# Keys turned through a memory scratch and a block turn on VectorE instead of on TensorE

## The chip, the cores and the metric

The kernel runs on one core of a Trainium2 chip. The time is the device time of one execution in microseconds; lower is better. Engines are called TensorE (PE, its weight loads PEld), VectorE (DVE), ScalarE (ACT), GpSimd (POOL) and SyncE (SP), which only issues DMAs here.

## The reference, cut to what matters

Input x has 16 sequences of 256 tokens with 512 features, in float32. Two stages follow each other, both with a gate and a residual:

```
k = layernorm(x)                       # per token, over 512 features
# per channel, over the 256 tokens of a sequence (a recurrence in time):
#   a <- decay * a + exp(k) * v ;  b <- decay * b + exp(k)
#   y = (a_prev + e2*exp(k)*v) / (b_prev + e2*exp(k))        v = ctx
x = x + tanh(g_xattn) * y
h = layernorm(x)
x = x + tanh(g_ffn) * (shared_mlp(h) + moe_top2_of_8(h))
```

Layernorm goes over features, so it wants tokens on the partitions. The recurrence goes over tokens, so it wants channels on the partitions and time along the row. Keys k and values v must therefore be transposed on the way in (tokens x channels to channels x tokens), and y on the way back.

## The kernel before

Tokens are cut into 32 tiles of 128 (512 features each); two tiles, one sequence, are a unit. The body walks over units 0 to 15 (and -2 and -1 as a lead-in without matmuls of the shared MLP); each unit has 11 steps, one for each 128-wide block of the shared MLP's hidden layer. Units 2 to 11 are a hardware loop of two units per turn, the others are written out. In step s of unit u TensorE makes `up_pair(u, s)` (24 matmuls, L1024) and, up to unit 13, `down_block(u-1, s-1)` (6 matmuls, L1057). Behind each `up_pair` stand ScalarE's Silu (L834), VectorE's product (`hidden`, L1311), ScalarE's rounding to float16 (`hidden_hi`, L850) and GpSimd's remainder (`hidden_lo`, L634). The Silu writes one of three staging buffers (`srng`) and waits until `hidden_lo` of three blocks earlier has read it; three PSUM buffers PU are used in turn too.

The attention stages of later units run in the same steps. Which step is written in the table `STAGE_AT`: for each stage, the offset in steps from the unit's own start, first and second tile. `-18` means 18 steps ahead, which is step 4 two units earlier. Every engine walks through the same steps and does its part of each stage in a fixed order within the step, so an instruction that waits holds back all that stands behind it on its engine. The stages of a tile:

- `stats_x`: VectorE's mean and variance of x (L1229, L1231); GpSimd's `inv_std` (L579, L581, L583) behind it in the same step.
- `norm_k`: ScalarE writes the normalised tile to `kbuf` (L798), the only such buffer.
- `turn_k`: TensorE transposes `kbuf` into PSUM bank PT with four matmuls (L948), ahead of the `up_pair` of its step; ScalarE's `exp_k` (L804) reads PT. PT is shared with the turned y.
- `factors` (GpSimd L595, L599), `turn_v` (values; by TensorE for the first two units, later from a load in blocks and VectorE's L1264), `den` (VectorE L1253 and the scan L1257; GpSimd's `add_den` L606), `num` (VectorE L1269 and the scan L1271; GpSimd's `add_num` L611), `divide` (VectorE L1276, L1279).
- `turn_y`: TensorE transposes y (L948) behind 18 of the 24 matmuls of an `up_pair`; it waits for `divide`. Then `add_y` (VectorE L1284), `norm_x2` (ScalarE L813, L814), `split_x` (VectorE L1293).
- SyncE turns and stores the row (`turn_and_store`, L422, L424), loads x two units ahead (L399); the transposed row is xT, which `logits` (TensorE L993) and `up_pair` read. `choose` (VectorE L1298 to L1305) picks the experts.

Of every second unit, the even ones from 2 on, GpSimd also sends eight indirect stores in steps 8, 9 and 10 (`send_slots`, L618: two, two and four), behind its `add_den` or `add_num` of that step. In unit 0 SyncE also loads the down weights (step 3 to 5) and writes 2560 KB of zeros to memory (L471, step 7). In units 12 to 14 VectorE and ScalarE also split weights of the first expert. From 767 us on come the experts' tiles.

How ctx comes in blocks already, for all units from 2 on (one DMA per quarter q of the partitions, four per tile, runs of 32 words):

```
sp.dma_start(ctxb[r][q * SQ:(q + 1) * SQ, :].rearrange("p (k b j) -> p k b j", k=KT, j=SQ),
             ctx_rows[bass.ds(c * P, P), :].rearrange("(b i) (k q j) -> q i k b j", i=SQ, k=KT, j=SQ)[q])
dve.transpose(PR[:, :], ctxb[k])
```

The load swaps 32x32 blocks, and VectorE's transposition, which turns each 32x32 block in itself, does the rest.

Of the kernel before, what the change touches and what calls it, by code (L numbers as in the profile page):

```python
# [9 lines left out]
P = 128  # L10
# [42 lines left out]
SQ = 32  # L53
# [4 lines left out]
STAGE_AT = {  # L58
    "stats_x": (-21, -16),
    "norm_k": (-19, -13),  # L60
    "turn_k": (-18, -12),
    "factors": (-16, -10),
    "turn_v": (-16, -10),
    "den": (-14, -9),
# [68 lines left out]

def tiles_at(stage, u, s):
    return [(u.shift(-(o // JT)), k) for k, o in enumerate(STAGE_AT[stage])
            if o % JT == s and u.shift(-(o // JT)).exists()]
# [6 lines left out]
def build(nc, x, ctx_in, g_x, g_f, t_decay, t_first, router, w_ug, w_dn, s_ug, s_dn, out):  # L143
    es = ExitStack()
    with es:
# [10 lines left out]
        moe_d = nc.dram_tensor("moe_d", (NTOK + 4 * P, D), F32, kind="Internal").ap()  # L156
        slot_d = nc.dram_tensor("slot_d", (TRASH + TOPK * NTOK, 2), F32, kind="Internal").ap()
# [155 lines left out]
        bn_done = [sem(f"bn{n}") for n in range(2)]; inv_done = [sem(f"inv{n}") for n in range(2)]  # L313
        k_norm = sem("k_norm"); k_turned = sem("k_turned"); v_turned = sem("v_turned"); v_used = sem("v_used")
# [76 lines left out]
        def _(sp):  # L391
# [8 lines left out]

            def load_ctx(c, r):
                if isinstance(c, int) and c < UT * PE_TURNED:
                    sp.dma_start(ctxb[r], ctx_rows[bass.ds(c * P, P), :]).then_inc(v_in[r], 16)
                else:
                    for q in range(P // SQ):
                        sp.dma_start(ctxb[r][q * SQ:(q + 1) * SQ, :].rearrange("p (k b j) -> p k b j", k=KT, j=SQ),
                                     ctx_rows[bass.ds(c * P, P), :].rearrange("(b i) (k q j) -> q i k b j", i=SQ, k=KT, j=SQ)[q]
                                     ).then_inc(v_in[r], 16)
# [39 lines left out]
            def unit(u, first=0):  # L448
                for s in range(first, JT):
                    if s == 1 and not (u.fixed and not 2 <= u.v < FIRST_HELD + 2):  # L450
                        start_sums(u.shift(-2))
                    for v, k in tiles_at("turn_v", u, s):
                        if v.shift(1).exists():
                            wait_alone(v_turned, v.tile(k) + 1)
                            load_ctx(v.tile(k) + 2, k)
                    for m in W_LOAD_AT.get(key(u, s), ()):
                        load_u(m)
                    for v, k in tiles_at("split_x", u, s):
                        turn_and_store(v, k)
                        if v.shift(2).exists():  # L460
                            if u.fixed and u.v in (1, 2):
                                sp.wait_ge(wd_lo, 5 if u.v == 1 and k == 0 else 6 if u.v == 1 else JT)
                                sp.wait_ge(wu_lo, JT)
                            load_x(v.shift(2), k)
                    if key(u, s) in EARLY_LOAD_AT:
                        load_chunk(0, EARLY_LOAD_AT[key(u, s)])
# [296 lines left out]
        def _(act):  # L763
# [91 lines left out]
            def unit(u, first=0, also=None):  # L855
                for s in range(first, JT):
# [4 lines left out]
                    for v, k in tiles_at("turn_k", u, s):  # L861
# [83 lines left out]
        def _(pe):  # L945
# [116 lines left out]
            def unit(u, first=0):  # L1062
                for s in range(first, JT):
                    for v, k in tiles_at("turn_k", u, s):
                        turn_k(v, k)

                    def attend():
                        for v, k in tiles_at("turn_v", u, s):
                            if v.fixed and v.v < PE_TURNED:
                                turn_v(v, k)  # L1070
# [125 lines left out]
        def _(dve):  # L1196
# [68 lines left out]

            def num(u, k):
# [165 lines left out]
            def unit(u, first=0, also=None):  # L1432
                for s in range(first, JT):
# [18 lines left out]
                    for v, k in tiles_at("split_x", u, s):  # L1452
                        split_x(v, k)
                    for v, k in tiles_at("divide", u, s):
                        divide(v.tile(k))
# [8 lines left out]
                    for v, k in tiles_at("turn_v", u, s):  # L1464
                        if not (v.fixed and v.v < PE_TURNED):
                            turn_v(v, k)
# [119 lines left out]
```

## Time and profile before

| | us |
|---|---|
| median of 3 runs | 1230.34 (1228.75 to 1232.13) |
| profiled execution, its own time | 1232.66 |
| its span, first to last instruction | 1230.9 |
| TensorE busy | 1163.2 (94%) |
| VectorE busy | 682.7 (55%) |
| GpSimd busy | 653.7 (53%) |
| ScalarE busy | 509.6 (41%) |
| TensorE's matmuls of unit 0, unit 1 begin | 50.57, 96.06 |
| last up_pair ends, about | 767 |

A timeline row gives the start, the time, the engine, the line, the operation, the tile written and those read, and in brackets how long the engine was idle before and which instruction ended that. Names are those of the allocation: `wkv` stands for all the attention buffers. One row can hold several instructions in a row of the same line (x4). Offsets are us from the span's start.

### The profile page before, as it was taken

What the parts mean: (1) busy time and instruction counts of PE and PEld (TensorE: products, weight loads), DVE (VectorE), ACT (ScalarE), POOL (GpSimd) and SP (SyncE); (2) the same over time, 40 slices, a digit from 0 to 9 for tenths busy, and PEclk for the clock granted to TensorE, in tenths of its full rate; (3) what the DMA queues carried; (4) which work ended last, traced back from release to release, by engine and by line L of the source; (5) the groups of instructions that cost most, each with busy time, mean ns of one, the idle gap of its engine ahead of it and who ended that gap; (6) DMA issues with size and microseconds to landing.
All of it is one profiled execution on the core that took longest, in us unless ns stands there. A gap on an engine that the chain in (4) does not pass through costs nothing. (4 is left out here: it accounts for less than half of the span.)

```text
span 1230.9 us, 25978 instructions
## 1 busy us (share of the span) xinstructions
PE 1163.2 (94%) x8396; PEld 817.2 (66%) x8396; DVE 682.7 (55%) x1357; ACT 509.6 (41%) x915; POOL 653.7 (53%) x754
## 2 busy tenths in 40 slices
PE   1478999999999999999999989999999999999998
PEld 1366777777777777777776767566666666666653
DVE  6776787786786777776777866222222223222112
ACT  5665444443544443544534443333333333333220
POOL 7887457367457457456557542344444444444320
PEclk9998999999999999999999989999999999999999
DMA  8373232232222222222332323999899989997738
GB/s 234 92 206 72 53 70 53 53 69 52 54 66 52 60 61 55 68 49 60 87 69 48 59 65 62 204 178 180 173 169 172 176 171 165 178 169 130 127 50 319
DMA packets 232773, 136.29 MB, mean 111 GB/s; under 512 B 176477, under 2 KB 201077, under 8 KB 232544
## 3 DMA queue, kind: packets, MB, share of 16 engines
q1 hardware_dynamic: 213792, 97.55, 34.3%
q0 software_dynamic: 18048, 37.47, 17.6%
q8 instruction: 51, 0.84, 0.3%
q14 instruction: 50, 0.41, 0.1%
q10 hardware_dynamic: 832, 0.02, 0.0%
HBM read 69.83 MB, written 44.97 MB: 93 GB/s over the span
## 5 line engine op out<-in xcount | busy, mean ns | idle before, releaser
L1024 PE MATMUL PU<-xT,wreg 128*128 128x256 f16 x4224 | 504.5, 276 | 0.4 <-DVE srng L1311 0.4
L1024 PEld LDWEIGHTS PU<-xT,wreg 128*128 128x128 f16 x4224 | 415.1, 99 | 74.8 <-DVE srng L1311 0.7
L753 POOL DMA_INDIRECT moe_d<-wkv,acc x71 | 112.0, 1578 | 217.2 <-ACT wkv L928 214.2
L1131 PE MATMUL PU<-acc,wkv 128*128 x1284 | 214.5, 312 | 0.0
L1057 PE MATMUL PD<-wreg,hreg 128*128 128x512 f16 x858 | 206.4, 379 | 0.0
L634 POOL TENSOR_TENSOR hreg<-srng,hreg 128x256 f16<-128x256 f32 x165 | 134.6, 822 | 73.9 <-ACT hreg L850 72.9
L1131 PEld LDWEIGHTS PU<-acc,wkv 128*128 128x128 f16 x1284 | 125.1, 97 | 69.4
L1545 DVE TENSOR_TENSOR wkv<-PR,wkv 128x384 f16<-128x384 f32 x71 | 39.6, 557 | 208.1 <-ACT wkv L922 148.7
L1152 PE MATMUL PD<-acc,wkv 128*128 (+1 forms) x639 | 149.6, 379 | 1.5 <-DVE wkv L1545 1.5
L834 ACT ACTIVATE srng<-PU 128x256 f32<-128x256 f32 x176 | 66.7, 379 | 201.4 <-PE PU L1024 149.5
L1057 PEld LDWEIGHTS PD<-wreg,hreg 128*128 128x128 f16 x858 | 84.0, 98 | 73.5
L850 ACT ACTIVATE hreg<-srng 128x256 f16<-128x256 f32 x176 | 72.5, 412 | 118.5 <-DVE srng L1311 117.1
L1311 DVE SCALAR_TENSOR_TENSOR srng<-PU,srng 128x256 f32<-128x256 f32 x176 | 72.5, 412 | 85.2 <-ACT srng L834 72.2
L1152 PEld LDWEIGHTS PD<-acc,wkv 128*128 128x128 f16 (+1 forms) x639 | 62.5, 98 | 67.7 <-issue 1.7
L1276 DVE RECIPROCAL wkv<-wkv 128x512 f32<-128x512 f32 x32 | 106.9, 3340 | 0.3
L928 ACT ACTIVATE wkv<-PD,acc 128x512 f32<-128x512 f32 x71 | 48.8, 687 | 106.6 <-PE PD L1152 81.4
L618 POOL DMA_INDIRECT slot_d<-stw,sidx x64 | 68.4, 1068 | 23.0 <-issue 15.8
L918 ACT ACTIVATE wkv<-PU 128x352 f32<-128x352 f32 x71 | 32.9, 463 | 113.4 <-PE PU L1131 47.2
L948 PE MATMUL PT<-ident,wkv 128*128 128x128 f32 x256 | 42.5, 292 | 38.9 <-ACT wkv L798 27.8
L606 POOL TENSOR_TENSOR wkv<-wkv 128x512 f32<-128x512 f32 x32 | 44.4, 1387 | 58.8 <-DVE wkv L1257 58.8
L1131 PE MATMUL PL<-acc,wkv 128*128 x420 | 68.4, 313 | 0.0
L948 PEld LDWEIGHTS PT<-ident,wkv 128*128 128x128 f32 x256 | 32.1, 149 | 48.4 <-ACT wkv L798 30.1
(177 smaller groups left out, 1327.5 us busy)
## 6 DMA issues: line engine op xcount, KB each, us to landing
wreg<-in_L_ffn_w_up_gate SPq DMA_DIRECT2D x48, 176.0 KB
acc<-in_x SPq DMA_DIRECT2D x32, 256.0 KB, 3.0
xhl_d<-wkv SPq DMA_DIRECT2D x32, 256.0 KB, 2.3
wkv<-in_ctx SPq DMA_DIRECT2D x112, 64.0 KB, 2.4
moe_d<-acc SPq DMA_DIRECT2D x13, 512.0 KB
out<-moe_d SPq DMA_DIRECT2D x2, 3328.0 KB, 21.1
acc<-n_L_ffn_shared_w_up_gate SPq DMA_DIRECT2D x16, 256.0 KB, 5.7
wreg<-in_L_ffn_w_down SPq DMA_DIRECT2D x12, 256.0 KB
```

The source lines that it names most:

```text
L618: pool.indirect_dma_start(out=slot_d, out_offset=bass.IndirectOffsetOnAxis(ap=sidx[:, 2 * (r.at + t) + k:2 * (r.at + t) + k + 1], axis=0), ...
L634: pool.tensor_tensor(hh[:, u.par, m, 1, :], srng[:, r, :], hh[:, u.par, m, 0, :], ALU.subtract).then_inc(hlo_ready, 1)
L753: pool.indirect_dma_start(out=moe_d, out_offset=bass.IndirectOffsetOnAxis(ap=didx[:, t:t + 1], axis=0), in_=ostage[t % 3], in_offset=None, ...
L834: act.activation(srng[:, r, :], PU[r][:, 0:UN], ACT.Silu, scale=1.0 / WS).then_inc(silu_done, 1)
L850: act.activation(hh[:, buf, m, 0, :], srng[:, r, :], ACT.Copy).then_inc(hhi_ready, 1)
L948: mm = pe.transpose(dst[:, kt * P:(kt + 1) * P], src[:, kt * P:(kt + 1) * P], ident[:, :])
L1024: mm = pe.matmul(PU[r][:, gu * UN:(gu + 1) * UN], sU[:, m, gu, a, kt, :], xT[:, u.par, b, kt, :], start=(kt == 0 and a + b == 0), stop=(kt ...
L1057: mm = pe.matmul(PD[t][:, :], hh[:, u.par, j, a, t * P:(t + 1) * P], sD[:, j, b, :], start=(j == 0 and a + b == 0), stop=(j == JT - 1 and ...
L1131: mm = pe.matmul(up_set[t % 2][gu][:, 0:I], xgT[:, t % 4, a, kt, :], weights(h, ((gu * 2 + b) * KT + kt) * I, P, I), start=(kt == 0 and a ...
L1152: mm = pe.matmul(PD[t % 2][:, :], ehT[0:M, t % 2, a, m * P:(m + 1) * P], weights(h, UW + (m * 2 + b) * D, M, D), start=(m == 0 and a + b = ...
L1276: dve.reciprocal(nd[:, 1], nd[:, 1]).then_inc(rcp_done, 1)
L1311: dve.scalar_tensor_tensor(out=srng[:, r, :], in0=PU[r][:, UN:2 * UN], scalar=HS / WS, in1=srng[:, r, :], op0=ALU.mult, op1=ALU.mult).then ...
```

## The change

From unit 2 on, keys take another way. `norm_k` writes `kbuf` as before. SyncE stores it to a scratch `k_d` in memory (`store_k`) and, when that has landed, loads it back into `kbuf` with its 32x32 blocks swapped (`load_k`, four DMAs, the same shape as for ctx). VectorE then turns the blocks into PT (`turn_k`), and `exp_k` reads PT as before. The four matmuls of `turn_k` on TensorE stay for units 0 and 1 alone. y is still turned by TensorE.

The longer way gets more steps: `stats_x`, with `inv_std`, moves from -21, -16 to -24, -20, `norm_k` from -19, -13 to -23, -18, and the key's turn from -18, -12 to -19, -13. `exp_k` keeps its step. The loads of ctx go one step later. In steps of the unit in which they run: `stats_x` from 1 and 6 to 9 and 2, `norm_k` from 3 and 9 to 10 and 4, the key's turn from 4 and 10 (TensorE) to 3 and 9 (VectorE). Units 0 and 1 keep the old table as `FIRST_AT`.

```diff
+FIRST_AT = {                       # units 0 and 1: the table of before
     "stats_x": (-21, -16), "norm_k": (-19, -13), "turn_k": (-18, -12),
+    "exp_k": (-18, -12), "load_v": (-16, -10), "store_k": (), "load_k": (),
...
 STAGE_AT = {
+    "stats_x": (-24, -20),
+    "norm_k": (-23, -18),
+    "store_k": (-23, -18),
+    "load_k": (-22, -17),
+    "turn_k": (-19, -13),
+    "exp_k": (-18, -12),
     "factors": (-16, -10),
     "turn_v": (-16, -10),
+    "load_v": (-15, -9),
...
+        k_d = nc.dram_tensor("k_d", (P, D), F32, kind="Internal").ap()
...
+            def load_blocks(buf, rows, landed):
+                for q in range(P // SQ):
+                    sp.dma_start(buf[q * SQ:(q + 1) * SQ, :].rearrange("p (k b j) -> p k b j", k=KT, j=SQ),
+                                 rows.rearrange("(b i) (k q j) -> q i k b j", i=SQ, k=KT, j=SQ)[q]).then_inc(landed, 16)
+            def store_k(c):
+                wait_alone(k_norm, c + 1)
+                sp.dma_start(k_d, kbuf).then_inc(k_out, 16)
+            def load_k(c):
+                wait_alone(k_out, 16 * (c + 1 - UT * PE_TURNED))
+                load_blocks(kbuf, k_d, k_in)
...
# SyncE, order within a step: start_sums, load_k, load_v, weights, turn_and_store with load_x, store_k, other loads
...
# TensorE
                     for v, k in tiles_at("turn_k", u, s):
-                        turn_k(v, k)
+                        if turned_by_pe(v):
+                            turn_k(v, k)
...
# VectorE, order within a step: hidden, add_y, choose, stats_x, split_x, turn_k, divide, den, num, turn_v
+            def turn_k(c):
+                wait_alone(k_in, 64 * (c + 1 - UT * PE_TURNED))
+                dve.wait_ge(x2_done, c - 1)
+                dve.transpose(PT[:, :], kbuf).then_inc(k_turned, 1)
```

## Rows read from the trace of the kernel before

**Rows 1.** TensorE's waits, whole span: line waited for, us in total, times, longest

```profile
PE PT L948 <- DVE wkv L1279: 11.1, 7, 3.5
```

**Rows 2.** busy us by stretch: PE, PEld, DVE, ACT, POOL, PEclk, DMA share, GB/s

```profile
426.00:471.00 45.00, 45.00 (x363) 34.30 (x361) 32.36 (x65) 18.06 (x33) 30.06 (x37) 1.00 0.25 59
```

**Rows 3.** timeline of TensorE, units 8 and 9: start, us, what

```profile
438.26 0.60 PE L948 MATMUL PT<-ident,wkv 128*128 128x128 f32 x4
...
456.31 0.60 PE L948 MATMUL PT<-ident,wkv 128*128 128x128 f32 x4
456.74 1.15 PE L1024 MATMUL PU<-xT,wreg 128*128 128x256 f16 x9
...
483.47 0.60 PE L948 MATMUL PT<-ident,wkv 128*128 128x128 f32 x4
```

**Rows 4.** timeline of VectorE, units 8 and 9, idle before in brackets

```profile
435.30 0.69 DVE L1279 TENSOR_TENSOR wkv<-wkv 128x512 f32<-128x512 f32 x1
...
437.46 0.17 DVE L1298 TENSOR_REDUCE lt<-PL 128x8 f32<-128x16 f32 x1 [1.13 <-PE PL L993]
...
444.03 0.69 DVE L1229 BATCH_NORM_STATS2 bn<-acc 128x6 f32 x1 [0.26 <-issue]
...
445.02 0.73 DVE L1264 STREAM_TRANSPOSE PR<-wkv 128x512 f32<-128x512 f32 x1
...
467.72 0.42 DVE L1311 SCALAR_TENSOR_TENSOR srng<-PU,srng 128x256 f32<-128x256 f32 x1 [4.48 <-ACT srng L834]
...
482.41 0.69 DVE L1279 TENSOR_TENSOR wkv<-wkv 128x512 f32<-128x512 f32 x1
```

**Rows 5.** timeline of GpSimd, unit 8 and the start of 9

```profile
445.50 0.22 POOL L579 TENSOR_SCALAR ve<-mv 128x1 f32<-128x1 f32 x1
...
446.58 0.27 POOL L583 TENSOR_SCALAR nmr<-mv,rstd 128x1 f32<-128x1 f32 x1 [0.21 <-POOL rstd L581]
...
452.20 1.18 POOL L606 TENSOR_TENSOR wkv<-wkv 128x512 f32<-128x512 f32 x1 [4.01 <-DVE wkv L1257]
...
457.28 1.18 POOL L611 TENSOR_TENSOR wkv<-wkv 128x512 f32<-128x512 f32 x1
...
466.53 1.30 POOL L634 TENSOR_TENSOR hreg<-srng,hreg 128x256 f16<-128x256 f32 x2
```

**Rows 6.** timeline of ScalarE, unit 8 step 8

```profile
451.30 0.38 ACT L834 ACTIVATE srng<-PU 128x256 f32<-128x256 f32 x1 [1.36 <-PE PU L1024]
```

**Rows 7.** two waits of TensorE and the granted clock (PEclk) behind them

```profile
66.39 0.66 PE L948 MATMUL PT<-ident,wkv 128*128 128x128 f32 x4 [1.31 <-ACT wkv L798]
...
73.62 0.79 PE L948 MATMUL PT<-ident,wkv 128*128 128x128 f32 x4 [1.80 <-DVE wkv L1279]
...
66.00:67.00 1.00, 0.61 (x6) 1.00 0.00 0
...
74.00:75.00 1.00, 1.00 (x7) 0.51 1.01 373
```

**Rows 8.** timelines of units -1 to 1: GpSimd, ScalarE, SyncE's queue, TensorE

```profile
51.52 1.18 POOL L611 TENSOR_TENSOR wkv<-wkv 128x512 f32<-128x512 f32 x1 [1.17 <-DVE wkv L1271]
...
48.92 0.58 ACT L804 ACTIVATE wkv<-PT 128x512 f32<-128x512 f32 x1
...
56.82 0.38 ACT L834 ACTIVATE srng<-PU 128x256 f32<-128x256 f32 x1 [3.98 <-PE PU L1024]
...
83.05 0.64 SPq L471 DMA_DIRECT2D moe_d<-hreg  x1
...
95.82 0.38 PE L993 MATMUL PL<-rt_w,xT 128*128 128x16 f16 x8 [6.52 <-DMA xT<-wkv]
```

**Rows 9.** DMA issues (KB each, median us to landing) and SyncE's issue time

```profile
xhl_d<-wkv SPq DMA_DIRECT2D x32, 256.0 KB, 2.3
wkv<-in_ctx SPq DMA_DIRECT2D x112, 64.0 KB, 2.4
...
473.80 2.98 SPq L406 DMA_DIRECT2D wkv<-in_ctx  x4
```

More of the change, by code:

```diff
@@ L57 @@
 LOOP = (1, 6)
-STAGE_AT = {
+FIRST_AT = {
     "stats_x": (-21, -16),
@@ L61 @@
     "turn_k": (-18, -12),
+    "exp_k": (-18, -12),
     "factors": (-16, -10),
     "turn_v": (-16, -10),
+    "load_v": (-16, -10),
+    "den": (-14, -9),
+    "num": (-13, -8),
+    "divide": (-12, -7),
+    "turn_y": (-11, -6),
+    "add_y": (-10, -5),
+    "norm_x2": (-9, -4),
+    "split_x": (-8, -3),
+    "logits": (-6, -1),
+    "choose": (-6, 1),
+    "store_k": (), "load_k": (),
+}
+STAGE_AT = {
+    "stats_x": (-24, -20),
[3 more added lines that the diff above has]
+    "turn_k": (-19, -13),
+    "exp_k": (-18, -12),
+    "factors": (-16, -10),
+    "turn_v": (-16, -10),
+    "load_v": (-15, -9),
     "den": (-14, -9),
@@ L131, with turned_by_pe @@
 LAST = [Route(GROUPS - 1, 14 * (GROUPS - 1), TILES - GT, UT, 0), Route(GROUPS, 14 * (GROUPS - 1) + 12, TILES - UT, UT, UT)]
+def turned_by_pe(u):
+    return u.fixed and u.v < PE_TURNED
 def tiles_at(stage, u, s):
-    return [(u.shift(-(o // JT)), k) for k, o in enumerate(STAGE_AT[stage])
-            if o % JT == s and u.shift(-(o // JT)).exists()]
+    found = []
+    for table, first in ((FIRST_AT, True), (STAGE_AT, False)):
+        for k, o in enumerate(table[stage]):
+            v = u.shift(-(o // JT))
+            if o % JT == s and v.exists() and turned_by_pe(v) == first:
+                found.append((v, k))
+    return found
 def key(u, s):
@@ L404, in load_ctx @@
                 else:
[L405 to L408, printed above, removed]
+                    load_blocks(ctxb[r], ctx_rows[bass.ds(c * P, P), :], v_in[r])
             def load_u(m):
@@ L451, in unit @@
                         start_sums(u.shift(-2))
-                    for v, k in tiles_at("turn_v", u, s):
+                    for v, k in tiles_at("load_k", u, s):
+                        load_k(v.tile(k))
+                    for v, k in tiles_at("load_v", u, s):
                         if v.shift(1).exists():
@@ L464, in unit @@
                             load_x(v.shift(2), k)
+                    for v, k in tiles_at("store_k", u, s):
+                        store_k(v.tile(k))
                     if key(u, s) in EARLY_LOAD_AT:
@@ L860, in unit @@
                         norm_k(v.tile(k))
-                    for v, k in tiles_at("turn_k", u, s):
+                    for v, k in tiles_at("exp_k", u, s):
                         exp_k(v.tile(k))
@@ L1453, in unit @@
                         split_x(v, k)
+                    for v, k in tiles_at("turn_k", u, s):
+                        if not turned_by_pe(v):
+                            turn_k(v.tile(k))
                     for v, k in tiles_at("divide", u, s):
@@ L1464, in unit @@
                     for v, k in tiles_at("turn_v", u, s):
-                        if not (v.fixed and v.v < PE_TURNED):
+                        if not turned_by_pe(v):
                             turn_v(v, k)
```

3 lines of the change are left out of this document (2 added, 1 removed).

## Prediction

> **What bounds the kernel now.** I first read the waits of TensorE, where the one for VectorE's y is the row to see [rows 1], and the busy table by stretches [rows 2]. In the loop TensorE has no gap at all: 45.00 of 45.00 us busy in a stretch of one unit, with VectorE at 32.36. All its large waits lie in units -2 to 1 and from unit 12 on. So any work taken off TensorE in units 1 to 13 is worth its full time, as long as nothing else ends last. I then read the timelines of each engine over unit 8 (matmuls from 416.94 us) and unit 9 (from 462.15), to see how far the other engines are from ending last, and found one place where they almost do. In step 5 of unit 9 TensorE starts to turn y at 483.47 [rows 3]; VectorE finished that y (L1279, 0.69 us) at 483.10 [rows 4]. The reserve is 0.37 us. The same place repeats in units 3, 5, 7, 9 and 11 (five times) with 0.23 to 0.37 us; step 5 of even units has 2.3 (438.26 against 435.99 [rows 3, 4]) and step 0 about 4.
>
> What makes this y late, followed back from 483.10: VectorE works without a real pause from 467.72, where it waited 4.48 us for the Silu [rows 4]. The Silu waited for the staging buffer that GpSimd's L634 frees at 466.53 + 0.65, and GpSimd was busy without a pause from 452.20 (`add_den` of step 8, then eight indirect stores of unit 8 with `add_num` among them) [rows 5]. That `add_den` waited until 452.20 for VectorE's scan, and VectorE had worked through from 437.46, where it last waited for TensorE, for the logits of unit 8 [rows 4]. From there to the y: 45.64 us. TensorE's own way between the same points: 46.01 us. The kernel has two nearly equal bounds.
>
> **The change part by part.**
>
> *Removed from TensorE:* 28 key turns, for tiles 4 to 31, made in units 0 to 13. One is 0.44 us of TensorE's time: it starts at 456.31 and the next matmul at 456.74 (0.43 to 0.44 wherever it stands) [rows 3]. Two per unit make 0.88 us, and 1.76 per pair of units. If TensorE stays the bound everywhere, 28 x 0.44 = 12.3 us.
>
> *Added to VectorE:* 28 block turns in steps 3 and 9. The same form exists for ctx: 0.73 us, and it holds the next instruction off for 0.63 to 0.73 [rows 4]. I take 0.65, with 0.95 as upper end for its two waits.
>
> *Moved:* `stats_x` leaves steps 1 and 6 for steps 9 and 2. On VectorE it holds 1.2 us (from the end of the one before to the transposition behind it, 443.8 to 445.02 [rows 4]). On GpSimd the three instructions of `inv_std` go with it, 1.35 us (445.50 to 446.85 [rows 5]). `norm_k` moves to steps 10 and 4 on ScalarE.
>
> *Along the late chain of a pair* (even unit 8, odd unit 9), against the times of before:
> VectorE, unit 8 steps 5 to 8: logits 0.44 earlier (one turn gone), `stats_x` gone from step 6, 1.2. The scan releases `add_den` at 450.55 instead of 452.20.
> VectorE, step 9: it must wait for the Silu of step 8, which starts at 451.30 [rows 6], now 0.44 earlier, so 451.3 for its product; then 0.3 product, 1.1 `stats_x`, 0.7 block turn, 0.7 multiply, 1.5 scan: 455.6. GpSimd, shifted with its `add_den`, is ready for `add_num` at 455.6 too: 1.6 earlier than 457.28 [rows 5].
> GpSimd then has `inv_std` of step 9 ahead of six indirect stores: +1.35. The staging buffer is free 0.25 us earlier than before.
> VectorE, unit 9 steps 1 to 4: step 1 loses `stats_x` and step 2 gains it, 0; step 3 gains the turn, +0.65.
> y is done at 483.10 - 0.25 + 0.65 = 483.5. TensorE, three key turns lighter, arrives at 483.47 - 1.32 = 482.15. It waits about 1.4 us (up to 1.7 with the dearer turn). The pair gains 1.76 - 1.4 = 0.3 us, where TensorE alone promised 1.76. The next y turns keep over 1 us of reserve (unit 8 step 5: 438.26 against 435.99 + 0.65).
> Five pairs, units 2 to 11: -1.5 us.
> Unit 1 has no indirect stores before it and 0.9 us of reserve: -0.88 + 0.2 = -0.7.
> Units 12 and 13: VectorE splits expert weights there too and TensorE waits for it already. The y turns of unit 13 step 5 and unit 14 step 0 are set by VectorE, +0.45 and +0.65: +1.1 together.
>
> *The first units.* Tile 4 now passes `norm_k` in unit -1 step 10, on ScalarE ahead of `exp_k` of tile 3, which it delays. GpSimd can give tile 4 its `inv_std` only behind `add_num` (51.52, now a `stats_x` of VectorE later, 52.6) [rows 8]: 53.8 + 1.35 = 55.1. ScalarE stands until then and has 0.8 us of `norm_k`, so `exp_k` of tile 3 goes from 48.92 to 55.9, 7.0 later. Behind it stand weight splitting and the first Silu, which had 3.98 us of idle time before it at 56.82 [rows 8]: it comes 3.0 later. VectorE's `stats_x` gone from step 1 gives a little back, so I take 2.7 us for tile 3's way. It ends in the transposition of its row into xT, for which TensorE waits 6.52 us at 95.82, because it stands behind the 2560 KB store of zeros issued at 83.05 [rows 8]. SyncE issues that store after its new waits (`store_k`, `load_k` behind the down weights), 1.5 to 3.2 us later. The wait swallows what the two turns gone from unit 0 save. I take +2.7, bounds 0 and +5.
>
> *SyncE and the DMA engines.* Per key tile one store and four loads more, 140 DMAs. A store of this size lands in 2.3 us, a ctx piece in 2.4; its four issues take 3.0 [rows 9]. The round trip is about 0.4 + 2.3 + 3.0 + 2.4 = 8.1 us, against 17 us from `norm_k` in step 10 (about 459) to the turn in step 3 (476). It is hidden; 0, and if the cover were gone the surplus would land on VectorE.
>
> **Sum:** -1.5 - 0.7 + 1.1 + 2.7 = +1.6 us. The profiled execution took 1232.66 with a span of 1230.9, the median of the runs is 1230.34; I add the sum to the median: 1232.0.
>
> **The rivals.**
> *Full gain.* VectorE's chain doesn't end last, because its turn or `inv_std` slips into pauses. For it: VectorE is busy only 72% of a unit [rows 2]. Against: the pauses lie outside this chain. Then 26 x 0.44 = 11.4 less 2.7 at the start: 1221.6. With half the wait: 1226.
> *The wait costs the clock too (slower).* After a wait of 1.31 us the granted clock stayed at 1.00, 2.4 GHz; after one of 1.80 us it fell to about 0.5, 1.2 GHz, and stayed there until 77.4 (the first of these us) [rows 7], which loses 1.7 us of work. My forecast of 1.4 to 1.7 lies between. From about 1.8 us of wait it decides: +1.7 in six pairs, 10 us: 1242. For it: each 0.1 us on the chain is in the wait. Against: the middle of my sum is nearer to 1.31.
> *The change doesn't do what it says for time:* the key trip comes late and VectorE stands in step 3. It needs twice the 8.1 us; each us late is 1 us per unit, 14 us: 1246.
>
> **How the numbers follow.** No difference, chain eats the gain: 0.47, own range 1227 to 1236. Full or half gain: 0.25. Clock falls in several pairs: 0.2. Late keys: 0.03. A dearer start alone (+5 or more): 0.05. The range for 8 in 10 reaches to 1222 and 1242. A measurement of this kernel tells 0.3%, 3.7 us, from no change. Faster: the gain cases and a little of the first, 0.28. Slower: clock, late keys, start and the upper edge of the first, 0.28. Within 0.3%: 0.44.
>
> **What would show it.** TensorE: 112 of the 272 matmuls of L948 gone; a wait "TensorE on L1279's line" of 1.2 to 1.7 us in step 5 of every odd unit from 3 on, none in the loop before; the spacing of two units 90.2 instead of 90.5. VectorE: 28 more transpositions of 0.73, now 56. Start: first matmul of unit 1 at 98 to 99 instead of 96.06. Wrong, if no such waits stand in the loop (then 1222), or if the granted clock shows 0.5 there (then 1242), or if VectorE waits for the key loads.

## The result: 29 us slower, and the profile after

| | before | after |
|---|---|---|
| median of six runs each | 1231.39 us | 1260.30 us |
| lowest to highest | 1228.75 to 1234.17 | 1258.53 to 1261.72 |
| span of the profiled execution | 1230.9 us | 1256.8 us |

The ratio is 1.0233, with a 95% interval of 1.0216 to 1.025. The time lies outside the range of 1222 to 1242 us. The profiled execution of the changed kernel took 1258.53 us. Lines have moved: turns by TensorE are L998, router logits L1043, up blocks L1074, down blocks L1107; VectorE's turn of ctx is L1315 and that of the keys L1320, the last multiplication of y L1335, `split_x` L1349, the second scan L1327; Silu is L884; GpSimd's `inv_std` is L629 to L633, `add_den` L656, an indirect store L668, `hidden_lo` L684.

TensorE's waits over the whole span (line waited for, us in total, times, longest):

```profile
PE PT L998 <- DVE wkv L1335: 29.9, 12, 4.7
PE PT L998 <- ACT wkv L848: 26.3, 4, 9.4
PE PL L1043 <- DMA xT<-wkv: 19.8, 7, 6.0
PE PU L1074 <- DVE srng L1367: 9.5, 8, 1.9
```

The wait for y went from 11.1 us [rows 1] to 29.9, and a wait of the up blocks for VectorE's hidden product, L1367, has come up that was 0.4 us before. The timeline of TensorE shows where both stand, here in unit 8's step 5 and in unit 9:

```profile
452.17 0.65 PE L998 MATMUL PT<-ident,wkv 128*128 128x128 f32 x4
...
478.11 0.82 PE L1074 MATMUL PU<-xT,wreg 128*128 128x256 f16 x6
480.08 2.79 PE L1074 MATMUL PU<-xT,wreg 128*128 128x256 f16 x24 [1.15 <-DVE srng L1367]
...
500.80 0.65 PE L998 MATMUL PT<-ident,wkv 128*128 128x128 f32 x4 [2.58 <-DVE wkv L1335]
```

Every pair of units in the loop has these two waits: 1.15 us at up block 1 of the odd unit (480.08) and about 2.55 us at the y turn of its step 5 (500.80, against 483.47 without a wait before [rows 3]). Even the y turn of step 5 of unit 8, which had 2.3 us of reserve [rows 3, 4], now starts only at 452.17, 0.13 us after its y.

The y turns of step 5 of units 3, 5, ..., 13 give the account, before and after: 212.04 and 217.62; 302.52 and 310.96; 393.00 and 405.90; 483.47 and 500.80; 573.95 and 594.02; 666.57 and 691.98. So 5.6 us are lost by unit 3, 14.5 in four pairs of the loop, 5.3 in units 12 and 13, and 0.5 behind them: 25.9 us, the difference of the two profiled spans. The medians differ by 28.9, because the profiled execution of the changed kernel was its fastest, and that of the kernel before, 1232.66 us, lay above its median. A pair of units was 90.48 us; now it is 93.2 to 93.3, or 94.9.

The difference between these two is the clock. Busy us by stretch (PE, PEld, DVE, ACT, POOL), PEclk, DMA share and GB/s, behind the y turn at 405.90 and behind the one at 500.80:

```profile
406.00:407.00 1.00, 1.00 (x10) 0.88 (x10) 0.59 (x5) 0.42 (x1) 0.37 (x1) 0.92 0.34 54
407.00:408.00 1.00, 1.00 (x4) 0.45 (x3) 0.49 (x3) 0.38 (x1) 1.00 (x2) 0.50 0.50 79
408.00:409.00 1.00, 1.00 (x4) 0.38 (x3) 0.96 (x2) 0.42 (x1) 1.00 (x2) 0.50 0.57 90
409.00:410.00 1.00, 1.00 (x5) 0.39 (x4) 0.69 (x1) 0.00 (x0) 0.29 (x1) 0.50 0.26 40
...
502.00:503.00 1.00, 1.00 (x6) 0.43 (x5) 0.73 (x4) 0.38 (x1) 1.00 (x2) 1.00 0.47 73
```

After the wait of 2.55 us that ended at 405.90 TensorE ran at 0.50, 1.2 GHz, for some 3.4 us. After the wait of 2.58 us that ended at 500.80 it stayed at 1.00. The clock fell at 311, 406, 594 and 669 us; before, not once between 110 and 690 us. A pair with a fall (94.9 us) is 1.7 us longer than the last pair of the loop, which has none (93.2).

Now the way of y back from 500.80. VectorE's timeline of unit 9 (idle before, in brackets), as far as it matters:

```profile
484.00 0.42 DVE L1367 SCALAR_TENSOR_TENSOR srng<-PU,srng 128x256 f32<-128x256 f32 x1 [2.66 <-ACT srng L884]
...
491.80 1.64 DVE L1349 TENSOR_TENSOR wkv<-wkv 128x512 f16<-128x512 f32 x1
493.37 0.71 DVE L1320 STREAM_TRANSPOSE PT<-wkv 128x512 f32<-128x512 f32 x1
494.00 0.66 DVE L1325 TENSOR_TENSOR wkv<-PR,wkv 128x512 f32<-128x512 f32 x1
494.69 1.67 DVE L1327 TENSOR_TENSOR_SCAN wkv<-wkv 128x516 f32<-128x516 f32 x1
...
499.98 0.69 DVE L1335 TENSOR_TENSOR wkv<-wkv 128x512 f32<-128x512 f32 x1
```

The block turn is the 0.71 us that was forecast. But `split_x`, 0.78 us at this place before, takes 1.64. GpSimd's timeline says what ran beside it:

```profile
471.62 1.18 POOL L661 TENSOR_TENSOR wkv<-wkv 128x512 f32<-128x512 f32 x1
472.89 0.23 POOL L629 TENSOR_SCALAR ve<-mv 128x1 f32<-128x1 f32 x1
...
473.98 0.66 POOL L633 TENSOR_SCALAR nmr<-mv,rstd 128x1 f32<-128x1 f32 x1 [0.21 <-POOL rstd L631]
474.80 1.08 POOL L668 DMA_INDIRECT slot_d<-stw,sidx  x1 [0.16 <-issue]
...
481.83 0.96 POOL L668 DMA_INDIRECT slot_d<-stw,sidx  x1 [0.30 <-issue]
482.81 1.30 POOL L684 TENSOR_TENSOR hreg<-srng,hreg 128x256 f16<-128x256 f32 x2
...
491.72 1.18 POOL L656 TENSOR_TENSOR wkv<-wkv 128x512 f32<-128x512 f32 x1 [2.96 <-DVE wkv L1308]
```

`add_den` starts at 491.72, 0.08 us ahead of `split_x`, and `split_x` is long by nearly the whole of it. In the kernel before, VectorE's `split_x` (L1293) and GpSimd's `hidden_lo` and `add_den` (L606) stood like this:

```profile
475.89 0.78 DVE L1293 TENSOR_TENSOR wkv<-wkv 128x512 f16<-128x512 f32 x1
```

```profile
474.49 1.63 POOL L634 TENSOR_TENSOR hreg<-srng,hreg 128x256 f16<-128x256 f32 x1
476.09 1.62 POOL L606 TENSOR_TENSOR wkv<-wkv 128x512 f32<-128x512 f32 x1
```

There `add_den` came 0.2 us behind `split_x`, because GpSimd still had a `hidden_lo` in hand; the `inv_std` that the change took out of step 1 had pushed that back. In the timeline of the changed kernel, the upper lines show the other part: `inv_std` of step 9 now stands behind `add_num` and ahead of six indirect stores, so the last store ends at 482.79 and `hidden_lo` frees the staging buffer only then. ScalarE shows who waits for which of the two:

```profile
474.84 0.81 ACT L848 ACTIVATE wkv<-acc,nmr,rstd 128x512 f32 x1 [5.28 <-POOL nmr L633]
475.67 1.28 ACT L854 ACT_TABLE_LOAD   x1
476.97 0.60 ACT L854 ACTIVATE wkv<-PT 128x512 f32<-128x512 f32 x1
477.46 0.41 ACT L900 ACTIVATE hreg<-srng 128x256 f16<-128x256 f32 x1
477.89 1.28 ACT L884 ACT_TABLE_LOAD   x1
479.18 0.38 ACT L884 ACTIVATE srng<-PU 128x256 f32<-128x256 f32 x1
...
483.58 0.38 ACT L884 ACTIVATE srng<-PU 128x256 f32<-128x256 f32 x1 [3.11 <-POOL hreg L684]
```

`norm_k` of step 10 stands 5.28 us for `inv_std` and everything behind it is late: Silu(10) at 479.18, its product on VectorE at 479.60, and TensorE's up block 1, which needs the PSUM buffer of block 10, at 480.08. Silu(0) at 483.58 waits for the staging buffer, and with it VectorE's whole odd unit.

The new transfers, in the table of DMA issues (KB each, median us to landing):

```profile
k_d<-wkv SPq DMA_DIRECT2D x28, 256.0 KB, 3.4
wkv<-k_d SPq DMA_DIRECT2D x112, 64.0 KB, 2.6
```

VectorE waits nowhere for them. The first units went as forecast: the first matmul of unit 1 starts at 99.11 instead of 96.06.

### The profile page after: what moved, and what is told of

Read it like the earlier page. It is cut to its first block and busy times, and to the rows that moved or that the text cites. A ratio compares the mean times of both kernels' runs of the same rounds, so it can differ in the third digit from the quotient of the medians.

```text
span 1256.8 us, 26058 instructions
## 1 busy us (share of the span) xinstructions
PE 1159.6 (92%) x8284; PEld 803.6 (64%) x8284; DVE 715.3 (57%) x1385; ACT 509.0 (41%) x915; POOL 630.1 (50%) x754
## 5 line engine op out<-in xcount | busy, mean ns | idle before, releaser
L1074 PE MATMUL PU<-xT,wreg 128*128 128x256 f16 x4224 | 506.6, 277 | 9.5 <-DVE srng L1367 9.5
L1074 PEld LDWEIGHTS PU<-xT,wreg 128*128 128x128 f16 x4224 | 414.7, 99 | 92.5 <-DVE srng L1367 10.0
L1107 PE MATMUL PD<-wreg,hreg 128*128 128x512 f16 x858 | 209.7, 384 | 0.0
L684 POOL TENSOR_TENSOR hreg<-srng,hreg 128x256 f16<-128x256 f32 x165 | 112.2, 685 | 91.9 <-ACT hreg L900 91.1
L1107 PEld LDWEIGHTS PD<-wreg,hreg 128*128 128x128 f16 x858 | 84.8, 99 | 75.8 <-issue 3.3
L1367 DVE SCALAR_TENSOR_TENSOR srng<-PU,srng 128x256 f32<-128x256 f32 x176 | 72.5, 412 | 98.9 <-ACT srng L884 96.0
L884 ACT ACTIVATE srng<-PU 128x256 f32<-128x256 f32 x176 | 66.4, 377 | 124.7 <-PE PU L1074 105.2
L656 POOL TENSOR_TENSOR wkv<-wkv 128x512 f32<-128x512 f32 x32 | 38.6, 1205 | 94.8 <-DVE wkv L1308 94.8
L668 POOL DMA_INDIRECT slot_d<-stw,sidx x64 | 69.1, 1080 | 22.5 <-issue 15.8
L998 PE MATMUL PT<-ident,wkv 128*128 128x128 f32 x144 | 26.8, 316 | 57.1 <-DVE wkv L1335 29.9
L848 ACT ACTIVATE wkv<-acc,nmr,rstd 128x512 f32 (+1 forms) x32 | 26.0, 813 | 87.7 <-POOL nmr L633 87.7
```

Source lines behind the costliest of these rows:

```text
L668: pool.indirect_dma_start(out=slot_d, out_offset=bass.IndirectOffsetOnAxis(ap=sidx[:, 2 * (r.at + t) + k:2 * (r.at + t) + k + 1], axis=0), ...
L684: pool.tensor_tensor(hh[:, u.par, m, 1, :], srng[:, r, :], hh[:, u.par, m, 0, :], ALU.subtract).then_inc(hlo_ready, 1)
L884: act.activation(srng[:, r, :], PU[r][:, 0:UN], ACT.Silu, scale=1.0 / WS).then_inc(silu_done, 1)
L1074: mm = pe.matmul(PU[r][:, gu * UN:(gu + 1) * UN], sU[:, m, gu, a, kt, :], xT[:, u.par, b, kt, :], start=(kt == 0 and a + b == 0), stop=(kt ...
L1107: mm = pe.matmul(PD[t][:, :], hh[:, u.par, j, a, t * P:(t + 1) * P], sD[:, j, b, :], start=(j == 0 and a + b == 0), stop=(j == JT - 1 and ...
L1367: dve.scalar_tensor_tensor(out=srng[:, r, :], in0=PU[r][:, UN:2 * UN], scalar=HS / WS, in1=srng[:, r, :], op0=ALU.mult, op1=ALU.mult).then ...
```

## The experiments

Twelve kernels ran beside these two. Each ratio compares a kernel with runs of the kernel before made beside it (their medians lie between 1230.74 and 1232.54 us). "y" and "up 1" are TensorE's waits at the y turn of step 5 and at up block 1 of an odd unit in the loop, "late way" is the time on VectorE from the reading of an even unit's logits (L1354, in unit 8 at 452.30) to the end of the odd unit's y, "falls" are stretches of granted clock at half between 110 and 690 us, and "a pair" is the time from one odd unit's y turn to the next one's, without and with a fall.

| kernel | us | ratio to before (95%) | y | up 1 | late way | a pair | falls |
|---|---|---|---|---|---|---|---|
| before | 1231.39 | | 0 | 0 | 45.64 | 90.48 | 0 |
| after | 1260.30 | 1.0233 (1.0216 to 1.0250) | 2.55 | 1.15 | 48.37 | 93.2; 94.9 | 4 |
| schedule alone | 1243.97 | 1.0097 (1.0078 to 1.0116) | 1.52 | 0 | 47.16 | 92.2 | 1 |
| no scratch | 1259.67 | 1.0219 (1.0199 to 1.0238) | 2.56 | 1.15 | 48.29 | 93.1; 94.9 | 5 |
| turn of 32 columns | 1244.39 | 1.0104 (1.0082 to 1.0125) | 1.90 | 0.74 | 47.50 | 91.9; 93.5 | 2 |
| statistics at old steps | 1233.19 | 1.0010 (1.0001 to 1.0020) | 1.14 | 0 | 46.06 | 90.1 | 1 |
| first tile's back | 1249.11 | 1.0144 (1.0129 to 1.0160) | 2.56 | 0 | 46.98 | 91.6; 94.5 | 3 |
| second tile's back | 1245.81 | 1.0108 (1.0092 to 1.0125) | 1.81 | 1.01 | 47.47 | 92.0; 93.6 | 2 |
| `add_den` behind `split_x` | 1249.56 | 1.0147 (1.0132 to 1.0162) | 1.35 | 1.15 | 47.00 | 92.3 to 92.6 | 1 |
| stores spread | 1239.23 | 1.0062 (1.0047 to 1.0078) | 0.67 | 1.15 | 46.33 | 91.4 | 0 |
| ScalarE's order | 1280.51 | 1.0403 (1.0387 to 1.0419) | 1.6; 2.5 | 0 | 49.65 | 97 to 98.4 | 5 |
| old steps, stores spread | 1226.51 | 0.9958 (0.9945 to 0.9972) | 0 | 0 | 44.76 | 88.8 | 1 |
| the same, two in a step | 1220.53 | 0.9906 (0.9889 to 0.9922) | 0 | 0 | 44.47 | 88.7 | 0 |
| before, stores spread | 1230.50 | 0.9987 (0.9978 to 0.9996) | 0 | 0 | 45.44 | 90.5 | 0 |

### Which part of the change costs it

**The schedule alone.** All tiles are turned by TensorE; the moved steps stay.

```diff
-    "store_k": (-23, -18),
-    "load_k": (-22, -17),
-    "turn_k": (-19, -13),
+    "store_k": (),
+    "load_k": (),
+    "turn_k": (-18, -12),
...
                     for v, k in tiles_at("turn_k", u, s):
-                        if turned_by_pe(v):
-                            turn_k(v, k)
+                        turn_k(v, k)
```

VectorE's call of `turn_k` is taken out with it.

> The changed kernel without its new turn: every key tile is turned by TensorE as before, nothing is stored to k_d or loaded from it, but statistics, key normalization and context loads keep the early steps that the change gave them. Theory A (the moved steps cost the time: inv_std comes behind add_num on GpSimd, norm_k sits ahead of the hidden product on ScalarE, and GpSimd meets VectorE's split_x and scan): most of the loss is here too, about 1245 to 1255 us, with waits at up block 1 of the odd unit. Theory B (the turn on VectorE costs it) and theory C (the new transfers cost it): within 3 us of the kernel before, about 1231 us.

1243.97 us, 1 us under theory A's range: 12 of 29 us, and without the waits at up block 1 in the loop that it expected. The y turn waits 1.52 us in each pair although VectorE turns no key, so the moved steps alone have used up the reserve of 0.37 us. The late way is 1.52 us longer than before, and `split_x` takes 1.65 us here too (at 484.15, with `add_den` at 484.06). Theories B and C, as the whole cause, are out.

**No trip through memory.** VectorE turns `kbuf` as it is, so the keys of tiles 4 to 31 are left with their blocks unswapped.

```diff
-                wait_alone(k_in, 64 * (c + 1 - UT * PE_TURNED))
+                wait_alone(k_norm, c + 1)
```

with `store_k` and `load_k` empty.

> The changed kernel without the trip through memory: VectorE turns kbuf itself as soon as it is normalized, so that the blocks of the key tiles from the loop on are not swapped and those keys are wrong; steps and turns are otherwise those of the changed kernel. Theory A and theory B: no change against the changed kernel, 1257 to 1262 us. Theory C (the store and the four loads of a tile delay SyncE's other transfers, or their contention does): at least 8 us less, near 1245 us or below.

1259.67 us, the same waits: the 140 transfers cost nothing that can be measured. Theory C has fallen.

**A turn of 32 columns.**

```diff
-                dve.transpose(PT[:, :], kbuf).then_inc(k_turned, 1)
+                dve.transpose(PT[:, 0:SQ], kbuf[:, 0:SQ]).then_inc(k_turned, 1)
```

> The changed kernel with VectorE's key turn cut from 512 to 32 columns; the other 480 columns of PT stay stale, so the keys are wrong. Everything else, the trip through memory and the waits too, is kept. The turn gets shorter by about 0.6 us in each of the 24 tiles. Theory A: 2 to 8 us less than the changed kernel, 1252 to 1258 us, with most of the wait of the y turn and all of the wait at up block 1 left. Theory B (what VectorE lost): at least two thirds of the loss goes, 1240 us or less.

1244.39 us: 16 us less than the changed kernel (28 turns are cut short, for tiles 4 to 31, not 24), twice what theory A allowed, and 55% of the loss where theory B wanted two thirds. Neither is right alone. The late way is 0.87 us shorter, the waits are 0.65 and 0.41 us shorter, and the falls go from 4 to 2. Once TensorE already waits, what VectorE's way gets shorter comes off the waits, and falls of the clock come off on top.

**The statistics at their old steps**, the rest as changed.

```diff
 STAGE_AT = {
-    "stats_x": (-24, -20),
+    "stats_x": (-27, -21),
```

> The changed kernel with one row of its table put back: stats_x (and GpSimd's inv_std with it) at offsets -27 and -21, so at steps 6 and 1 as before instead of 9 and 2; the key normalization stays at 10 and 4, the trip and VectorE's turn stay. Theory A: the waits at up block 1 of the odd unit go, the y turn waits about 1.4 us at most, no fall of the clock in the loop: 1230 to 1238 us. Theory B and theory C: 1255 to 1262 us, as the changed kernel.

1233.19 us. This one line of the table takes 27 of the 29 us away, with the trip and the turns in place. TensorE's wait in the loop, and the pair of instructions that ran long in the changed kernel, first VectorE, then GpSimd:

```profile
482.59 0.65 PE L998 MATMUL PT<-ident,wkv 128*128 128x128 f32 x4 [1.13 <-DVE wkv L1335]
```

```profile
474.61 0.78 DVE L1349 TENSOR_TENSOR wkv<-wkv 128x512 f16<-128x512 f32 x1
```

```profile
473.21 1.63 POOL L684 TENSOR_TENSOR hreg<-srng,hreg 128x256 f16<-128x256 f32 x1
474.81 1.63 POOL L656 TENSOR_TENSOR wkv<-wkv 128x512 f32<-128x512 f32 x1
```

Here `split_x` starts first and takes 0.78 us, as before the change, and it is `add_den` that runs long, where nothing waits for it at once.

### Which of the moved steps, and by which way

**The first tile's statistics back.**

```diff
-    "stats_x": (-24, -20),
+    "stats_x": (-27, -20),
```

> The changed kernel with the statistics of the first tile of a unit alone put back (offset -27, step 6); those of the second stay at -20, step 2. Theory D: only the inv_std of step 9 stands ahead of the indirect stores, so the wait at up block 1 goes and the wait at the y turn shrinks to 1.1 to 1.8 us: 1232 to 1242 us. Rival (the inv_std of step 2, which meets split_x and the scan of step 3, carries the greater part): 1246 us or more.

1249.11 us, outside theory D's forecast and in the rival's range: step 2 carries the greater part. The wait at up block 1 is gone, as forecast; the one at the y turn is still 2.56 us. So the other tile followed.

**The second tile's statistics back.**

```diff
-    "stats_x": (-24, -20),
+    "stats_x": (-24, -21),
```

> The changed kernel with the statistics of the second tile of a unit alone put back (offset -21, step 1); those of the first stay at -24, step 9. Theory E (two separate costs: the inv_std of step 9 holds norm_k and with it Silu(10), 1.15 us at up block 1; and the statistics in step 2 let GpSimd's add_den start just ahead of VectorE's split_x, which makes the y turn late by a further 0.9 to 1.4 us and brings the falls of the clock): a wait of 1.15 us at up block 1 and one of 1.0 to 1.5 us at the y turn in each pair, no fall of the clock before 650 us, 1238 to 1244 us. Rival (the two waits make up for each other, and the longer chain behind the indirect stores sets the pair whichever tile is moved): a wait of 2.5 us at the y turn again, 1248 us or more.

1245.81 us. The two waits of a pair, from TensorE's timeline:

```profile
472.59 2.79 PE L1074 MATMUL PU<-xT,wreg 128*128 128x256 f16 x24 [1.01 <-DVE srng L1367]
492.41 0.65 PE L998 MATMUL PT<-ident,wkv 128*128 128x128 f32 x4 [1.82 <-DVE wkv L1335]
```

The y wait is longer than the 1.0 to 1.5 of theory E and well under the rival's 2.5, the time is 2 us over theory E's range, and a fall of the clock came at 306 us that it had ruled out. The late way sorts it out. With both tiles' statistics at the old steps it takes 46.06 us; moving the second adds 0.92 (46.98), moving the first adds 1.41 (47.47), moving both 2.31 (48.37), their sum. The first move acts through GpSimd's stores, whose last one ends 29.1 us after the logits are read in the two kernels without it and 30.5 in the two with it. The second acts in step 3, `split_x` 1.64 against 0.78 us. Theory E had overlooked that the first one's 1.4 us reach the y turn too, beyond what TensorE has lost at up block 1.

**`add_den` held back.** GpSimd starts it in step 2 only after `split_x`:

```diff
                     for v, k in tiles_at("den", u, s):
+                        if k == 1 and not (u.fixed and u.v < 1):
+                            wait_alone(xlo_ready, v.tile(0) + 1)
                         add_den(v.tile(k))
```

> The changed kernel with one wait added on GpSimd: in step 2 add_den of the second tile starts only when VectorE has done split_x, so that the two no longer run over each other. Theory E: split_x takes 0.68 to 0.78 us there instead of 1.64, the wait at the y turn shrinks from 2.55 to about 1.7 us, and one to four falls of the clock go with it; 1248 to 1256 us. Rival (split_x is stretched by something else, or the time it gives back is lost again behind the later add_den): 1258 us or more.

1249.56 us, 10.7 less by one more wait on GpSimd. VectorE's timeline at the place of the two long instructions, and GpSimd's:

```profile
487.25 0.68 DVE L1351 TENSOR_TENSOR wkv<-wkv 128x512 f16<-128x512 f32 x1
487.85 0.72 DVE L1322 STREAM_TRANSPOSE PT<-wkv 128x512 f32<-128x512 f32 x1
488.48 0.67 DVE L1327 TENSOR_TENSOR wkv<-PR,wkv 128x512 f32<-128x512 f32 x1
489.18 1.27 DVE L1329 TENSOR_TENSOR_SCAN wkv<-wkv 128x516 f32<-128x516 f32 x1
```

```profile
488.18 1.18 POOL L656 TENSOR_TENSOR wkv<-wkv 128x512 f32<-128x512 f32 x1 [3.98 <-DVE wkv L1351]
```

`split_x` is at 0.68 and the scan at 1.27 instead of 1.67, and `add_den` runs beside the block turn and the multiplication from PSUM without lengthening either. The y wait is 1.35 us and the clock doesn't fall before 661 us; of the 10.7 us, three falls fewer are some 5. The held `add_den` isn't free: at the y turn of step 0, where TensorE didn't wait in the changed kernel's loop, it now waits 0.5 to 0.7 us for `exp_k` (L856). That it is the order of the two instructions that stretches `split_x` is shown.

**The indirect stores spread**: two each in steps 8 and 9 of the even unit and 0 and 1 of the odd one.

```diff
+SEND_AT = {(0, 8): 0, (0, 9): 1, (1, 0): 2, (1, 1): 3}
...
-                    if u.par == 0 and s > 7 and not (u.fixed and (u.v < 2 or u.v == UNITS - 2)):
-                        for t in ((0,), (1,), (2, 3))[s - 8]:
-                            send_slots(group_route(u.half - 1), t)
+                    w = u if u.par == 0 else u.shift(-1)
+                    if w.exists() and not (u.fixed and (w.v < 2 or w.v == UNITS - 2)):
+                        t = SEND_AT.get((u.par, s))
+                        if t is not None:
+                            send_slots(group_route(w.half - 1), t)
```

> The changed kernel with the eight indirect stores of a pair spread: two each in steps 8 and 9 of the even unit and in steps 0 and 1 of the odd one, instead of 2, 2 and 4 in steps 8, 9 and 10. Its moved steps, the trip and VectorE's turn stay. Theory D: the wait at the y turn of the odd unit falls from 2.55 us to 0.7 or less and the clock no longer falls in the loop; the 1.15 us at up block 1 stay, since norm_k still waits for inv_std behind add_num: 1236 to 1246 us. Rival (the y turn is late by VectorE's own work: the turn, and split_x and the scan stretched beside GpSimd): 0 to 5 us less than the changed kernel, 1255 to 1260 us.

1239.23 us, as theory D has it: y 0.67 us, up block 1 untouched at 1.15, no fall of the clock. The trace adds one thing: `split_x` isn't mended here. It takes 1.91 us (at 481.14), held by a `hidden_lo` that runs until 481.36 and by the `add_den` that follows it without a gap. The gain comes from the staging buffer, which GpSimd frees earlier: VectorE begins its odd unit 29.0 us after the reading of the logits instead of 31.7.

**ScalarE's order.**

```diff
-                    for v, k in tiles_at("norm_k", u, s):
-                        norm_k(v.tile(k))
-                    for v, k in tiles_at("exp_k", u, s):
-                        exp_k(v.tile(k))
...
+                    def keys():
+                        for v, k in tiles_at("norm_k", u, s):
+                            norm_k(v.tile(k))
+                        for v, k in tiles_at("exp_k", u, s):
+                            exp_k(v.tile(k))
...
+                    if s != 10:
+                        keys()
...
                         hidden_silu(u, s)
+                    if s == 10:
+                        keys()
```

> The changed kernel with one order turned round on ScalarE: in step 10 the two activations of the hidden product come before norm_k and exp_k instead of behind them. Theory D (the pair is set by GpSimd: inv_std of the first tile stands ahead of the indirect stores of steps 9 and 10, and with them hidden_lo(9), Silu(0) and the rest of VectorE's odd unit come late): the wait of 1.15 us at up block 1 of the odd unit goes, and the wait at the y turn grows by as much, because the last indirect store ends when it did; 1256 to 1262 us. Rival (norm_k ahead of Silu on ScalarE is a cost by itself): 1.15 us in each of six pairs and with it the falls of the clock, 1245 to 1253 us.

1280.51 us; both were wrong. The wait at up block 1 went, but the block of `norm_k`, table load and exponential now stands ahead of Silu(0), and the table for Silu can be loaded again only after the wait for the staging buffer. ScalarE and VectorE there:

```profile
496.63 1.28 ACT L884 ACT_TABLE_LOAD   x1 [5.71 <-POOL hreg L684]
497.92 0.38 ACT L884 ACTIVATE srng<-PU 128x256 f32<-128x256 f32 x1
```

```profile
498.33 0.42 DVE L1373 SCALAR_TENSOR_TENSOR srng<-PU,srng 128x256 f32<-128x256 f32 x1 [8.51 <-ACT srng L884]
```

So the load of 1.28 us came onto the late way, which is 49.65 us instead of 48.37. It also opened waits for xT of 2.6 us and for the even unit's y of 1.0 to 1.1 us in each pair, which I did not follow further.

### A version that beats both

**Old steps and spread stores**: `"stats_x": (-27, -21)` and `SEND_AT`, both as above.

> Both: stats_x at its old steps (offsets -27 and -21) and the eight indirect stores spread over steps 8, 9, 0 and 1, the rest as in the changed kernel. Theory D: no wait of TensorE over 0.5 us between 110 and 660 us, and 24 turns of 0.44 us off its queue: 1220 to 1228 us, faster than the kernel before. Rival: like the run with the statistics alone put back, 1231 to 1235 us, with the wait of 1.14 us in every pair.

1226.51 us: no wait in the loop, a pair in 88.77 us. In unit 13 a wait of 2.20 us stood at the y turn, and VectorE's timeline with GpSimd's shows why:

```profile
650.38 0.67 DVE L1328 TENSOR_TENSOR wkv<-PR,wkv 128x512 f32<-128x512 f32 x1
651.08 2.94 DVE L1330 TENSOR_TENSOR_SCAN wkv<-wkv 128x516 f32<-128x516 f32 x1
```

```profile
650.12 0.97 POOL L669 DMA_INDIRECT slot_d<-stw,sidx  x1 [0.30 <-issue]
651.11 0.68 POOL L685 TENSOR_TENSOR hreg<-srng,hreg 128x256 f16<-128x256 f32 x1
651.74 1.19 POOL L657 TENSOR_TENSOR wkv<-wkv 128x512 f32<-128x512 f32 x1
```

The stores in step 1 had pushed `hidden_lo` and `add_den` onto the scan, and it was held for both of them. In every odd unit of the loop (3 to 11) the same scan took 2.94 us too, without a wait of TensorE.

**Two stores in a step**, one line changed against the version above:

```diff
-SEND_AT = {(0, 8): 0, (0, 9): 1, (1, 0): 2, (1, 1): 3}
+SEND_AT = {(0, 8): 0, (0, 9): 1, (0, 10): 2, (1, 0): 3}
```

> The version with the statistics at their old steps and the stores spread, with the stores in four steps in a row: 8, 9 and 10 of the even unit and 0 of the odd one, two in each, so that none runs ahead of add_den in step 1 of the odd unit, where VectorE's second scan took 2.94 us instead of 1.23 us. Theory: the scan goes back to 1.2 to 1.6 us; in the loop nothing waited, so it stays at 88.8 us a pair, and the wait of 2.20 us in unit 13 shrinks: 1223 to 1226 us. Rival (stores in step 10 make Silu(0) of the odd unit late again and open a wait at the y turn): 1227 us or more.

1220.53 us, 0.94% faster than before (0.78 to 1.11%), and better than forecast. The scan in unit 9 is back at 1.52 us. TensorE's y turns of step 5 of units 7 and 9, with nothing in brackets:

```profile
389.23 0.60 PE L1001 MATMUL PT<-ident,wkv 128*128 128x128 f32 x4
...
477.96 0.60 PE L1001 MATMUL PT<-ident,wkv 128*128 128x128 f32 x4
```

88.73 us apart, and so are those of units 11 and 13 (566.69, 655.41): 1.75 us a pair less than before, which is four turns of 0.44. The 6 us to the version above are in the main the wait of 2.20 us and two falls of the clock, at 659 and 744 us, that are gone.

**The kernel before with the stores spread**: the same edit as in the changed kernel, with `SEND_AT = {(0, 8): 0, (0, 9): 1, (1, 0): 2, (1, 1): 3}`.

> The kernel before, with nothing of the change, and only the eight indirect stores of a pair spread over steps 8, 9, 0 and 1. It has no wait of TensorE in the loop that the stores could shorten. Theory D: no change, 1229 to 1233 us, so that what the version with the turn on VectorE, the statistics at their old steps and the stores spread wins is due to the turns taken off TensorE. Rival (the spread stores are worth their few us in any kernel): 1224 to 1228 us.

1230.50 us, inside theory D's range: by the ratio 0.13% less than before (0.04 to 0.22%), so the spread stores are worth next to nothing by themselves. They paid in the two kernels in which TensorE waited for VectorE's y, 21 us in the changed kernel and 7 with the statistics at their old steps. The order of the best version, two stores in each of four steps in a row, was not tried in the kernel before.

## Why the prediction was wrong

**What held.** 112 of the 272 matmuls of the turns are gone. One turn is 0.44 us of TensorE, and four of them 1.75 us in a pair, as the best version shows. The turn on VectorE takes 0.72 us. The transfers are hidden. The start lost 3.05 us where 2.7 were forecast, by the way described. That VectorE and TensorE are two nearly equal bounds held too, and so did the price of a fall of the clock, 1.7 forecast and 1.6 to 1.8 measured.

**The step that failed** is the late way of a pair, in two of its lines.

"VectorE, unit 9 steps 1 to 4: step 1 loses `stats_x` and step 2 gains it, 0." In VectorE's own instructions it is 0, but the move takes `inv_std` out of GpSimd's step 1 and so lets `add_den` start 0.08 us ahead of `split_x` instead of behind it. That cost 0.9 us on the late way in each pair: 0.92 between the kernels with both tiles' and with the first tile's statistics back, 0.90 between the changed kernel and the one with the second tile's back. The kernel with `add_den` held back shows that it is the order that does it.

"GpSimd then has `inv_std` of step 9 ahead of six indirect stores: +1.35. The staging buffer is free 0.25 us earlier than before." The forecast also has the logits 0.44 us earlier, so counted from their reading, as below, it has the buffer free 0.19 us later; it was 1.44 later. From `add_den` to the last store it was 2.0 us longer, not 1.35, with `inv_std` taking 1.75 us there. And the 1.2 us that should have been won ahead of it, `stats_x` gone from step 6, shrank to 0.55: two instructions of slot counting (L1457, 453.58 to 455.62) took 2.04 us instead of 0.5. In the trace they stand beside GpSimd's two `factors` instructions (L645 and L649, 453.53 to 455.57, without a gap), as `split_x` stands beside `add_den`; before, they began only when these were nearly done. The same 2.03 us stand in the kernels with the statistics at their old steps, the best one too, and 1.04 and 0.84 us in the one in which TensorE turns every key. So neither the steps of the statistics nor VectorE's turn brings them about alone; which of the other moves does was not tested.

So y came 2.73 us later after the logits than before, where the forecast's own terms give 0.84 (0.4 later by the clock, with the logits 0.44 earlier). TensorE's wait became 2.55 us instead of 1.4.

**What was not seen.** I followed `norm_k` into step 10 for the first units, where it delayed `exp_k` and Silu, but not for the loop. There it holds Silu(10), and up block 1 of the next unit waits 1.15 us for its PSUM buffer. And "the next y turns keep over 1 us of reserve" failed: unit 8's has 0.13 us. Between the first matmul of unit 1 and the y turn of unit 3 the changed kernel lost 2.5 us more, where the forecast has it gain about 1 (-0.7 for unit 1, -0.3 for the pair): the waits are already there, 1.00 us at 124.70, 1.07 at 196.90, 1.40 at 215.12 for xT, and 1.14 at 217.62.

**The account of the loop**, four pairs from unit 3 to 11: -7.0 for the turns, +10.2 at the y turns, +4.6 at up block 1, +3.4 for two falls of the clock, 11.2 together of 14.5. Most of the rest is at the waits themselves. Laid beside the best version, the pair of units 8 and 9 loses 1.35 us at the wait of 1.15 and 2.9 at that of 2.58, and 0.2 at the even y turn, which shows no wait: some 0.7 us more than the records say. About half of that is overlap: where nothing stops, a row of TensorE's timeline begins 0.16 to 0.17 us before the one ahead of it ends, and a wait is counted from that end only. The rest is small delays that I did not take apart.

**The rivals.** "The wait costs the clock too" named something that came, four falls in the loop and the two units behind it at the price forecast for one, but at waits of 2.55 us; it left out that a longer wait costs its own length, and the waits weigh more than the falls (14.8 against 3.4 us in four pairs). The forecast for the loop, 1.4 us of wait and 90.2 us a pair, is near what the kernel with the statistics at their old steps shows: 1.14 us, 90.1 us, 1233.19 us. That fits its sum, in which the moved statistics nearly cancel (-1.2 and +1.35 us). So the turn was priced about right, and the moved statistics were not. "Full gain", 1221.6 us, was not wrong as a limit: another kernel, with the order on GpSimd mended, reaches it.

**Left open.** Units 12 and 13 lost 5.3 us instead of 1.1; part are the same two waits with two falls, the rest was not taken apart. The waits for xT in the kernel with ScalarE's order turned, and the 1.40 us one at 215.12, have no cause here. And the same wait of 2.55 us was followed by a fall of the clock at 311, 406 and 594 us and not at 500.80; with the first tile's statistics back, at 491 and 586 and not at 308 and 400.

## What to carry to other kernels

Where two engines are nearly equal bounds, taking work off one pays only as far as the other's way has reserve. Count the reserve in order of time across every engine of that way, and follow each moved instruction on all the engines that it queues on, in the loop as well as at the start. A step that is moved at no cost in busy time can change which of two instructions starts first, and that alone was worth 0.9 us a pair here. After an offload, look again at what now ends last: the same spread of stores was worth at most 2.7 us before it and, with the steps put back, some 7 us after it, and 13 in its better order.

## What the hardware showed

VectorE's instructions with two inputs in SBUF and GpSimd's ran one after the other, whichever started first. `split_x` took 1.64 us when `add_den` (1.18 us) had started 0.08 us earlier, 0.68 to 0.78 us when it hadn't; in the other order `add_den` took 1.63 us. A scan of 1.23 us took 2.94 beside two GpSimd instructions of 0.68 and 1.19 us that followed each other without a gap, behind a store that ended as it began: it did not get in between them. Nor did `split_x` with 1.91 us behind a `hidden_lo` and an `add_den` (stores spread, at 481.14); but in the kernel before (at 475.89, 0.78 us) it got in between the same two. What decides that no run shows. The block turn (one input in SBUF) and a multiplication from PSUM kept their 0.72 and 0.67 us beside the same `add_den`. One input alone doesn't decide it: in the kernel before, a small cast (L1305) took 0.99 us at 438.57 beside `factors`, and 0.17 at 471.44. The Trainium skill, "SBUF — State Buffer", section "SBUF: two separate sides", states this as an exclusive lock on a shared pair of ports, held for the whole instruction, which counts for a VectorE instruction with two SBUF inputs against a GpSimd one that reads SBUF; the traces here agree.

The granted clock fell to half after some single waits of TensorE, mostly for about 3.4 us. After the waits of 2.5 to 2.6 us in the loop it fell in 8 cases of 12 (changed kernel, no scratch, first tile's statistics back), once while the wait was still on; after those of 1.8 to 1.9 us once in five and once in four (second tile's back, turn of 32 columns); after waits of 1.5 us and less at the y turn with nothing else near, not once. A fall of 3.4 us costs 1.6 to 1.8 us. One of 6.8 us, from 490.9 with the first tile's statistics back, cost 3.0: that pair took 94.5 us and the one ahead of it 91.5.
